# Softmax queries and keys in three bf16 parts instead of two f32r parts, and error attention's loads spread over a batch

## The chip, the cores and the metric

The kernel runs on one core of a Trainium2 chip. The metric is the device time of one execution in microseconds (us); each kernel is timed in several executions and their median is compared. The engines are TensorE (PE), VectorE (DVE), ScalarE (ACT), GpSimd (POOL) and SyncE (SP); SP here issues nearly all transfers, which run on 16 DMA engines.

## The reference, cut to what matters

The input is x of shape (4, 512, 128): four batches (b = 0..3) of 512 tokens. The model adds to x, in this order, half a feed-forward layer with ternary weights, an attention layer, half a feed-forward layer again, half a top-1 mixture of experts, a linear attention, and half the mixture of experts again. The change is in the attention layer, where v is the normalised input itself (16 heads of 8 columns):

```python
scores = jnp.einsum('bhqd,bhkd->bhqk', q, k) * scale          # 16 heads of 8
scores = jnp.where(causal, scores, -jnp.inf)
y_ar = jnp.einsum('bhqk,bhkd->bhqd', jax.nn.softmax(scores, axis=-1), v)
e = v[:, :, 1:, :] - y_ar[:, :, :-1, :]                       # the error of the first attention
...
ma = jnp.einsum('bhqd,bhkd->bhqk', qa, ka)                    # qa from q, ka from other keys, no softmax
ma = jnp.where(jnp.tril(jnp.ones((t - 1, t - 1), dtype=bool)), ma, 0.0)
y_ma = jnp.einsum('bhqk,bhkd->bhqd', ma, e)
out = merge(y_ar) @ w_proj.T + b_proj + (merge(y_ma) @ w_proj.T + b_proj)
```

The softmax is over large scores, so q and k have to enter the products at nearly f32 precision, and the largest score of each query is needed before the exponentials.

## The kernel before, in words

A batch's 512 tokens are NT = 4 tiles of 128. The 16 heads are worked in NS = 4 sets of HL = 4 heads (`hs` = 0..3).

**Split and stack.** PE projects q and k of a batch, ACT copies them to `qf` and `kf` (128 rows, 512 columns). DVE rounds them to f32r (`split`, L1153), POOL subtracts to get the low part (`low`, L590 to L592, called by `low_parts`). SP writes the parts to DRAM with `stack` (L363 to L366), three DMAs of 256 KB for q and three for k, in the orders (high, low, high) and (high, high, low), so that one head has 3 x 8 rows that belong together: high with high, low with high, high with low. A fourth block of 8 rows a head is zero or one, written once at the start (L356 to L361) and used for the row of maxima. The same is done for the features of error attention (`keep_features`). `keep_softmax` and `keep_features` are called batch by batch in SP's program, between the loads of the first sets.

**Sets.** SP loads a set from DRAM, once with queries as weights for the maxima (`load_max_set`, L376 to L382, ring halves 2 and 3) and once with keys as weights for the exponentials (`load_exp_set`, L368 to L374, ring halves 0 and 1): one operand stacked in 128 rows, the other in a block-diagonal ring whose other rows POOL has cleared (`clear_ring`, L573 to L576). A matmul of 128 queries by 4 heads x 128 keys (or the reverse) then gives four heads' scores at once. Maxima: ten such units a set go to PSUM banks, with a causal mask added by a bf16 matmul where the tile is on the diagonal; DVE reduces each (`maxima`, L1164, or two at once, `wide_maxima`, L1173, for the first batch). `max_of_tiles` (L1177 to L1184) joins the tiles, PE turns the result (`max_turn`), ACT copies it (`max_t`), and SP puts the maxima into the ring as the 25th row of a head (`max_row`, L412 to L414; for the very first set ACT does, L941), so that the scores come out with the maximum subtracted.

**Order around the change.** The order of all engines is written out by hand. Ahead of attention: projections and splits of the four batches, the maxima of batch 0, `max_of_tiles(0)`, the first scores. SP's program there is: values and softmax parts of batch 0, the first two maximum sets, features of batch 0, softmax parts and features of batch 1, softmax parts of batch 2, third maximum set, features of batch 2, fourth maximum set, batch 3. In attention, set by set, PE does the scores of a set, the answers of the set before and the maxima of the same set of the next batch; ACT does five exponentials a set (L900), POOL zeroes what is above the diagonals (`clear_late`, L655 to L660), and answers start a set with tile 0's eight matmuls. The last batch has no maxima beside it. At a batch's start SP loads all that error attention needs (`load_state`, L391 to L396: queries 4 x 192 KB, keys 1 MB, the next tokens' values 256 KB) and then the next batch's values (`load_values`, L398 to L402, which waits until the values before have been copied). Error attention of a batch follows its fourth set.

Of the kernel before, what the change touches and what calls it, by code (L numbers as in the profile page):

```python
# [92 lines left out]
SEMS = """held loaded experts_loaded first_loaded xt_low w_abs w_sum w_scale w_half w_low  # L93
w_tern zeroed pad_zero stats moments var_eps rstd normed xt_mm xt_ready x2_mm x2_ready ffn_h ffn_act
ffn_out ffn_base ffn_x x_in0 x_in1 x_in2 x_in3 qkv_mm proj_evac split_hi split_lo q_kept k_kept xset0 xset1 mset0 mset1 v_kept v_in ma_q ma_k
ma_hi ma_lo mq_kept mk_kept state_in ka_t_mm ka_tok v_aug smax_mm smax_red max_t
# [8 lines left out]
MAX_PAIRS = [(qt, kt) for qt in range(NT) for kt in range(qt + 1)]  # L105
EXP_PAIRS = [(kt, qt) for kt in range(NT) for qt in range(kt, NT)]
EXP_UNITS = [((0, 0), (0, 1)), ((0, 2), (0, 3)), ((2, 2), (3, 3)), ((1, 1), (2, 3)), ((1, 2), (1, 3))]
# [9 lines left out]
def build(nc, x_in, bias_cols, w_attn_t, w_k2_t, w_proj_t, b_proj, w1_t, w2_t, b2,  # L117
          l1_w, l1_bv, l1_wp, l1_bp, wr, mw1, mw2, consts, out):
    ctx = ExitStack()
    with ctx:  # L120
# [8 lines left out]
        def unit_slots(i):  # L129
            a, b = (slot_of[pair] for pair in EXP_UNITS[i])  # L130
            return banks[:, a:b + 1:b - a]
# [52 lines left out]
        with nc.sbuf_tensor("sb_xsets", [P, 2, T], F32R) as x_sets:  # L184
            pass
# [10 lines left out]
        yT = w1  # L196
        qs = sb("qs", [P, 2, T], F32R)
        ks = sb("ks", [P, 2, T], F32R)
# [6 lines left out]
        with nc.sbuf_tensor("sb_wide_rows", [P, B, NT, RW], F32) as wide_rows:  # L205
            pass
        ring = sb("ring", [P, NS, HL, T], F32R)
        with nc.sbuf_tensor("sb_v_low", [P, 2, T], F32) as v_low:
            pass
        m_sets = sb("m_sets", [P, 2, T], F32R)  # L210
# [30 lines left out]
        mpart = sb("mpart", [P, NS, NPAIR, HL])  # L241
        mneg = sb("mneg", [P, NT, H])
        mT = qs[0:H, 0]
# [23 lines left out]
        def dram(name, shape):  # L267
            return nc.dram_tensor(name, shape, F32, kind="Internal").ap()

        q_scr = dram("q_scr", [B, H, 4, HD, T])  # L270
        k_scr = dram("k_scr", [B, H, 4, HD, T])
# [14 lines left out]
        def head_rows(scr, b, h, n):  # L286

            return scr[b, h].rearrange("c d t -> (c d) t")[0:n]

        def set_rows(scr, b, hs):  # L290

            return scr[b, HL * hs:HL * hs + HL].rearrange("h c d t -> (h c d) t")
# [43 lines left out]
        def _(sp):  # L336
# [18 lines left out]
            by_set = last_rows(k_scr).rearrange("(s h) d t -> s h d t", h=HL)  # L355
            for dst in (last_rows(q_scr), last_rows(mk_scr), last_rows(k_scr)[:, 1:HD]):  # L356
                n = dst.shape[0] * dst.shape[1] * dst.shape[2] // P
                sp.dma_start(dst, zero[:, 0:n]).then_inc(s["pad_zero"], 16)
            sp.dma_start(by_set[:, 1:HL, 0], zero[0:(HL - 1) * B * NS, 0:T]).then_inc(s["pad_zero"], 16)
            sp.wait_ge(s["zeroed"], 2)  # L360
            sp.dma_start(by_set[:, 0, 0], v_next[0:B * NS].rearrange("p t d -> p (t d)")).then_inc(s["pad_zero"], 16)  # L361
# [5 lines left out]

            def load_exp_set(b, hs):  # L368

                i, done = hs % 2, s[f"xset{hs % 2}"]  # L370
                for hl in range(HL):
                    sp.dma_start(ring[VW * hl:VW * hl + 3 * HD, i, hl].bitcast(F32),
                                 head_rows(q_scr, b, HL * hs + hl, 3 * HD)).then_inc(done, 16)
                sp.dma_start(x_sets[:, i].bitcast(F32), set_rows(k_scr, b, hs)).then_inc(done, 16)  # L374

            def load_max_set(b, hs):  # L376

                i, done = hs % 2, s[f"mset{hs % 2}"]
                for hl in range(HL):
# [4 lines left out]
            def load_features(pad, b, done_q, done_k):  # L384

                for hl in range(HL):
                    dst = pad[VW * hl:VW * hl + 3 * HD, :, hl]
                    sp.dma_start(dst.bitcast(F32), heads(mq_scr[b], hl)).then_inc(done_q, 16)
                sp.dma_start(ka_stk[:].bitcast(F32), sets(mk_scr[b])).then_inc(done_k, 16)

            def load_state(b):  # L391

                hold(sp, s["ym_mm"], NT * b)
                load_features(qa_pad[:].rearrange("p (s h) t -> p s h t", s=NS), b, s["state_in"], s["state_in"])
                sp.dma_start(v_next[:, 0:NT - 1], v_scr[b, 1:T - P + 1].rearrange("(t p) d -> p t d", p=P)).then_inc(s["state_in"], 16)
                sp.dma_start(v_next[0:P - 1, NT - 1], v_scr[b, T - P + 1:T]).then_inc(s["state_in"], 16)  # L396

            def load_values(b):  # L398

                if b:  # L400
                    hold(sp, s["v_aug"], b)
                sp.dma_start(values_of[b % 2][:], v_scr[b].rearrange("(t p) d -> p t d", p=P)).then_inc(s["v_in"], 16)  # L402
# [9 lines left out]
            def max_row(b, hs):  # L412

                sp.dma_start(ring[3 * HD:3 * HD + 1, hs % 2].bitcast(F32),  # L414
                             mT[HL * hs:HL * hs + HL].bitcast(F32)).then_inc(s[f"xset{hs % 2}"], 16)
# [8 lines left out]
            def keep_softmax(b):  # L424

                hold(sp, s["split_lo"], 2 * b + 1)
                stack(qs, q_scr[b], s["q_kept"], (0, 1, 0))
                hold(sp, s["split_lo"], 2 * b + 2)
                stack(ks, k_scr[b], s["k_kept"], (0, 0, 1))
# [8 lines left out]
            sp.wait_ge(s["pad_zero"], 80)  # L438
# [3 lines left out]
            hold(sp, s["q_kept"], 48)  # L442
            hold(sp, s["k_kept"], 48)
# [15 lines left out]
            for kept in ("q_kept", "k_kept"):  # L459
                hold(sp, s[kept], 48 * B)  # L460
            next_max_set(0, 2)
            hold(sp, s["ffn_h"], NF * B)
# [107 lines left out]
        def _(pool):  # L570
            pool.memset(e_pad[:], 0.0).then_inc(s["zeroed"], 1)
            pool.memset(v_next[:], 1.0).then_inc(s["zeroed"], 1)
            pool.memset(carry[:], 0.0).then_inc(s["zeroed"], 1)  # L573
            def clear_ring(first, last):

                pool.memset(ring[:, first:last].bitcast(F32), 0.0).then_inc(s["zeroed"], 1)  # L576
# [17 lines left out]
            def scatter(m, b, first=0, last=NT):  # L594
# [3 lines left out]
                if b == 0 and first == 0:  # L598
                    pool.wait_ge(s["pad_zero"], 80)
# [63 lines left out]
            def errors(b, hs):  # L663

                pool.wait_ge(s["y_norm"], NS * b + hs + 1)
                if hs == 0:
                    pool.wait_ge(s["state_in"], 112 * b + 112)
# [35 lines left out]
            clear_ring(0, 2)  # L703
# [10 lines left out]
            clear_ring(2, 3)  # L714
# [5 lines left out]
            clear_ring(3, 4)  # L720
# [3 lines left out]
            for b in range(1, B):  # L724
                before_attention(b)
            low_parts(B - 1)
# [63 lines left out]
        def _(act):  # L790
# [68 lines left out]
            def max_t(b):  # L859
# [5 lines left out]
                else:  # L865
                    act.wait_ge(s["q_kept"], 48 * B)
# [1244 lines left out]
```

## Time and profile before

| what | value |
|---|---|
| median of 3 executions | 621.57 us (620.26 to 624.51) |
| the profiled execution | 621.04 us |
| its span | 619.2 us |
| mean granted clock of PE | 0.948 |
| PE busy | 505.4 us (82%) |
| DVE busy | 342.3 us (55%) |
| POOL busy | 243.5 us (39%) |
| ACT busy | 214.8 us (35%) |
| DMA | 79.85 MB, mean 129 GB/s |

The span is the time from the first to the last recorded instruction; the rest of the execution's time lies around it. A busy share is an average over stages with different limits, so a stage's limit is read from that stage. The granted clock is PE's, as a share of full speed (2.4 GHz; the lower of its two levels is 1.2 GHz), averaged over a stretch.

### The profile page before, as it was taken

The page shows a single profiled execution, that of the slowest core. Times are in us where ns is not written, and L with a number is a line of the kernel's source. Part 1 is how long each engine was busy: PE and PEld are TensorE (multiplying, and loading weights), DVE is VectorE, ACT ScalarE, POOL GpSimd, SP SyncE. Part 2 cuts the span into 40 slices and gives each one's busy share as a digit, 9 for nine tenths or more (in the row PEclk, how much of TensorE's full clock was granted, in tenths as well). Part 3 has the DMA queues.
Part 4 walks back from the last instruction along what each step waited for, and adds up shares of the span by engine and source line. Part 5 has one row for each costly group of instructions (what it writes and reads, how often), then busy time and mean ns, then how long its engine had stood idle before and what let it go on. Part 6 is the DMA issues. An engine that isn't in the chain of part 4 may idle for free.

```text
span 619.2 us, 10399 instructions
## 1 busy us (share of the span) xinstructions
PE 505.4 (82%) x3827; PEld 322.3 (52%) x3827; DVE 342.3 (55%) x912; ACT 214.8 (35%) x298; POOL 243.5 (39%) x292
## 2 busy tenths in 40 slices
PE   1787787989999999987888878965887788788893
PEld 0664333434644644462467744962456566563692
DVE  5654585648487757751144760323696888842131
ACT  1346331644455455445643701202231311110120
POOL 5667464223342334235332467452220220323153
PEclk9998797989999999998999999997998989977997
DMA  7306999733263263225299523312756273110220
GB/s 261 146 23 198 311 279 298 195 117 95 69 188 96 62 158 118 58 45 155 71 174 217 165 86 111 94 40 72 201 183 187 74 201 111 54 51 35 86 63 10
DMA packets 73666, 79.85 MB, mean 129 GB/s; under 512 B 10946, under 2 KB 50499, under 8 KB 73360
## 3 DMA queue, kind: packets, MB, share of 16 engines
q1 hardware_dynamic: 70760, 73.15, 42.6%
q0 software_dynamic: 2560, 5.58, 2.6%
q8 instruction: 31, 0.51, 0.4%
q10 hardware_dynamic: 296, 0.47, 0.2%
q14 instruction: 19, 0.16, 0.1%
HBM read 44.07 MB, written 35.72 MB: 129 GB/s over the span
## 4 chain that ended last, share of the span: by engine, by line
PE 49%; DVE 17%; SPq 8%; DMA 7%; POOL 7%; issue 6%; ACT 5%; POOLq 0%; DVEq 0%; ACTq 0%
PE ps_accum L1505 15%; PE ps_pair L1505 15%; PE ps_max_pair L1505 13%; SPq L366 3%; POOL sb_rstd L583 2%; DVE sb_stats L1061 2%; DVE sb_work L1400 2%; DMA sb_v_next<-v_scr 2%; DVE sb_mpart L1164 2%; SPq L380 1%; SPq L402 1%; PE ps_turn L1513 1%; POOL xe_scr L603 1%; PE ps_max_pair L1513 1%; DVE sb_mv L1064 1%
## 5 line engine op out<-in xcount | busy, mean ns | idle before, releaser
L1164 DVE TENSOR_REDUCE sb_mpart<-ps_max_pair 128x4 f32<-128x512 f32 x132 | 88.0, 688 | 47.1 <-PE ps_max_pair L1505 46.7
L900 ACT ACTIVATE sb_work<-ps_pair 128x1024 f32<-128x1024 f32 x80 | 80.9, 1024 | 71.3 <-PE ps_pair L1505 70.5
L1505 PE MATMUL ps_max_pair<-sb_ring,sb_m_sets 128*128 128x512 f32 x146 | 64.8, 471 | 7.6 <-DVE sb_mpart L1164 4.6
L660 POOL TENSOR_SCALAR_AFFINE_SELECT sb_work<-sb_work 128x512 f32<-128x512 f32 (+1 forms) x48 | 37.7, 789 | 72.1 <-ACT sb_work L900 72.1
L1505 PE MATMUL ps_pair<-sb_ring,sb_xsets 128*128 128x512 f32 x160 | 58.7, 455 | 8.9 <-DMA sb_ring<-sb_qs 3.7
L1505 PE MATMUL ps_pair<-sb_ident_bf,sb_ones_bf 128*128 128x512 bf16 x185 | 50.6, 431 | 12.3 <-DMA sb_x<-y_scr 8.0
L1505 PE MATMUL ps_accum<-sb_work,sb_v_aug 128*32 128x128 f32 (+3 forms) x768 | 59.3, 408 | 1.1 <-POOL sb_work L660 1.1
L1505 PEld LDWEIGHTS ps_max_pair<-sb_ring,sb_m_sets 128*128 128x128 f32 x146 | 26.9, 191 | 45.1 <-DVE sb_mpart L1164 28.7
L1505 PEld LDWEIGHTS ps_pair<-sb_ring,sb_xsets 128*128 128x128 f32 x160 | 29.0, 200 | 22.6 <-DMA sb_ring<-sb_qs 7.1
L1400 DVE TENSOR_TENSOR sb_work<-ps_pair,sb_cst 128x1024 f32<-128x1024 f32 x32 | 37.5, 1214 | 2.6 <-PE ps_pair L1505 2.6
L1505 PEld LDWEIGHTS ps_pair<-sb_ident_bf,sb_ones_bf 128*128 128x128 bf16 x185 | 19.9, 110 | 36.3 <-issue 11.7
L603 POOL DMA_INDIRECT xe_scr<-sb_exit_rows,sb_slot_all x16 | 15.9, 996 | 54.5 <-DVE sb_slot_all L1145 50.9
L581 POOL TENSOR_SCALAR sb_ve<-sb_mv 128x4 f32<-128x4 f32 x24 | 5.5, 229 | 68.9 <-DVE sb_mv L1064 63.8
L1505 PE MATMUL ps_pair<-sb_y_tmp,sb_mw 128*128 128x256 f32 x128 | 30.7, 383 | 2.0 <-ACT sb_y_tmp L962 2.0
L1505 PEld LDWEIGHTS ps_accum<-sb_work,sb_v_aug 128*32 128x32 f32 x768 | 18.0, 115 | 24.9 <-issue 19.5
L1505 PE MATMUL ps_pair<-sb_xs,sb_w1r 128*128 128x512 f32 x64 | 22.3, 474 | 9.2 <-DVE sb_xs L1080 5.6
L1344 DVE TENSOR_SCALAR sb_work<-ps_pair 128x512 f32<-128x512 f32 x16 | 10.9, 682 | 27.5 <-PE ps_pair L1505 27.5
L1505 PEld LDWEIGHTS ps_pair<-sb_y_tmp,sb_mw 128*128 128x128 f32 x128 | 23.1, 190 | 5.5 <-ACT sb_y_tmp L962 3.0
L583 POOL TENSOR_TENSOR sb_rstd<-sb_ve,sb_cst 128x4 f32<-128x4 f32 x24 | 25.0, 1040 | 2.0
L1505 PE MATMUL ps_pair<-sb_ring,sb_ka_stk 128*128 128x512 f32 x64 | 22.3, 463 | 2.9 <-DVE sb_work L1400 2.8
L679 POOL TENSOR_SCALAR_AFFINE_SELECT sb_work<-sb_work 128x1024 f32<-128x1024 f32 x16 | 17.4, 1091 | 17.5 <-ACT sb_work L891 17.5
L1006 ACT COPY sb_y_tmp<-ps_accum 128x512 f32<-128x512 f32 x16 | 9.4, 586 | 39.8 <-PE ps_accum L1505 39.8
(251 smaller groups left out, 994.6 us busy)
## 6 DMA issues: line engine op xcount, KB each, us to landing
sb_expert_rows<-xe_scr SPq DMA_DIRECT2D x16, 258.0 KB, 2.8
sb_m_sets<-q_scr SPq DMA_DIRECT2D x16, 256.0 KB
sb_ka_stk<-mk_scr SPq DMA_DIRECT2D x4, 1024.0 KB
xe_scr<-sb_cst SPq DMA_DIRECT2D x4, 1024.0 KB, 12.8
sb_mw<-in_mw SPq DMA_DIRECT2D x16, 256.0 KB, 5.9
sb_ka_stk<-mk_scr SPq DMA_DIRECT2D x8, 512.0 KB
sb_xsets<-k_scr SPq DMA_DIRECT2D x15, 256.0 KB
q_scr<-sb_qs SPq DMA_DIRECT2D x12, 256.0 KB, 3.7
```

Of the source, the lines that this page charges most:

```text
L366: sp.dma_start(scr[:, c], hi_lo[:, part, :].bitcast(F32)).then_inc(kept, 16)
L583: pool.tensor_tensor(rstd[i][:], ve[i][:], const("minus_half"), ALU.pow).then_inc(s["rstd"], 1)
L603: pool.indirect_dma_start(xe_scr[m], bass.IndirectOffsetOnAxis(ap=slot_all[:, i:i + 1], axis=0), rows_out[m][b][:, t, :], None).then_inc(s ...
L660: pool.affine_select(weights, weights, [[0, weights.shape[1]], [0, HL], [1, P]], ALU.is_ge, 0.0, base=0, channel_multiplier=-1).then_inc(s ...
L679: pool.affine_select(part, part, [[0, 2 * HL], [1, P]], ALU.is_ge, 0.0, base=-1, channel_multiplier=-1).then_inc(s["ma_zeroed"], 1)
L900: act.activation(unit_slots(i), pair[u % 2][:], ACT.Exp, scale=SCALE).then_inc(s["exp_done"], 1)
L1061: dve.bn_stats(stats[i][:, t, :], src[:, t, :]).then_inc(s["stats"], 1)
L1164: dve.tensor_reduce(mpart[:, m // NPAIR, m % NPAIR, :], max_banks[m % 2][:].rearrange("p (h k) -> p h k", h=HL), AX.X, ALU.max).then_inc(s ...
L1344: dve.tensor_scalar(work[:, n % 2, 1, :], pair[n % 2][:, 1, :], 0.0, None, ALU.max).then_inc(s["h_relu_v"], 1)
L1400: dve.tensor_tensor(work[:, n % 4].rearrange("p a (h q) -> p (a h) q", h=HL), pair[n % 2][:].rearrange("p a (h q) -> p (a h) q", h=HL), bc ...
L1505: return pe.matmul(dst, lhsT, rhs, start=start, stop=stop, skip_group_check=True)
L1513: last = pe.transpose(tile(dst, t), src[:, t, 0:D], ident)
```

## The change

Parts: q and k are split in three bf16 parts each (a, b, c, from high to low). Six products are kept, aa, ab, ac, ba, bb, ca, so a head has 48 rows in place of 24 and two rows of maxima (a bf16 part and the rest) in place of one. Two heads fill 128 rows, at rows 0 and 64, so a set's operands are two head pairs side by side (`x_sets`, `m_sets`, and the rings `x_ring`, `m_ring`, all bf16). PE does as many columns as before, some of them in matmuls of 256.

DVE writes the first part, and POOL's `low_parts` does the rest in six operations, which now wait for DVE's `query_features` as well, since POOL subtracts in place in `qf`. SP writes six DMAs of 128 KB each for q and for k in place of three of 256 KB, loads a set with four DMAs (384 KB in all) in place of five (448 KB), and a row of maxima with two in place of one. Of the zero blocks in DRAM only that of error attention's keys is still written at the start. POOL clears `x_ring` in place of the ring's first half and, behind each of the two other pieces of the ring, half of `m_ring`; it fills `x_sets` with ones before the last batch's split.

Error attention's loads: at a batch's start only the next tokens' values are loaded; the queries come around the maximum set behind set 0, the keys in two halves and the next batch's values behind set 1.

The order of exponentials' units changes in two places: units 2 and 3 are ((2,2),(2,3)) and ((1,1),(3,3)) in place of ((2,2),(3,3)) and ((1,1),(2,3)). `max_of_tiles` gets two more small operations, which split the maxima in two parts.

```diff
+PARTS = 6
+HP = 2
+PR = P // HP
-EXP_UNITS = [((0, 0), (0, 1)), ((0, 2), (0, 3)), ((2, 2), (3, 3)), ((1, 1), (2, 3)), ((1, 2), (1, 3))]
+EXP_UNITS = [((0, 0), (0, 1)), ((0, 2), (0, 3)), ((2, 2), (2, 3)), ((1, 1), (3, 3)), ((1, 2), (1, 3))]
...
+            def stack_queries(b):
+                for c0, c1, part in ((0, 3, 0), (3, 5, 1), (5, 6, 2)):
+                    for c in range(c0, c1):
+                        sp.dma_start(q_scr[b][:, c], q_parts[:, part]).then_inc(s["q_kept"], 16)
+            def stack_keys(b):
+                for c, part in enumerate((0, 1, 2, 0, 1, 0)):
+                    sp.dma_start(k_scr[b][:, c], k_parts[:, part]).then_inc(s["k_kept"], 16)
             def load_max_set(b, hs):
...
-                for hl in range(HL):
-                    sp.dma_start(ring[VW * hl:VW * hl + 3 * HD, 2 + i, hl].bitcast(F32),
-                                 head_rows(k_scr, b, HL * hs + hl, 3 * HD)).then_inc(done, 16)
-                sp.dma_start(m_sets[:, i].bitcast(F32), set_rows(q_scr, b, hs)).then_inc(done, 16)
+                for j in range(HP):
+                    rows_of = slice(PR * j, PR * j + PARTS * HD)
+                    sp.dma_start(m_ring[rows_of, i, :, j], half_rows(k_scr, b, hs, j)).then_inc(done, 16)
+                    sp.dma_start(m_sets[rows_of, i], half_rows(q_scr, b, hs, j)).then_inc(done, 16)
...
             for b in range(B):
-                load_state(b)
-                if b + 1 < B:
-                    load_values(b + 1)
+                load_next_values(b)
                 for hs in range(NS):
...
+                    if hs == 0:
+                        load_queries(b, 0, 2)
                     if b + 1 < B:
                         next_max_set(b + 1, hs)
+                    if hs == 0:
+                        load_queries(b, 2, HL)
+                    elif hs == 1:
+                        load_keys(b, 0, 2)
+                        load_keys(b, 2, NS)
+                        if b + 1 < B:
+                            load_values(b + 1)
...
             def low_parts(b):
-                low(s["split_lo"], qf[:], qs, s["split_hi"], 2 * b + 1)
-                low(s["split_lo"], kf[:], ks, s["split_hi"], 2 * b + 2)
+                operands = ((qf, q_parts), (kf, k_parts))
+                for i, (full, parts) in enumerate(operands):
+                    pool.wait_ge(s["split_hi"], 2 * b + i + 1)
+                    if i == 0:
+                        pool.wait_ge(s["ma_q"], b + 1)
+                    pool.tensor_tensor(full[:], full[:], parts[:, 0], ALU.subtract).then_inc(s["split_part"], 1)
+                for i, (full, parts) in enumerate(operands):
+                    pool.wait_ge(s["split_part"], 4 * b + i + 1)
+                    pool.tensor_copy(parts[:, 1], full[:]).then_inc(s["split_part"], 1)
+                for i, (full, parts) in enumerate(operands):
+                    pool.wait_ge(s["split_part"], 4 * b + i + 3)
+                    pool.tensor_tensor(parts[:, 2], full[:], parts[:, 1], ALU.subtract).then_inc(s["split_lo"], 1)
...
-            clear_ring(2, 3)
+            pool.memset(ring[:, 2].bitcast(F32), 0.0)
+            clear(m_ring[:, 0])
...
-            clear_ring(3, 4)
+            pool.memset(ring[:, 3].bitcast(F32), 0.0)
+            clear(m_ring[:, 1])
...
                 if b:
                     split(b - 1, 0)
+                    query_features(b - 1)
                     split(b - 1, 1)
-                    query_features(b - 1)
...
             def max_of_tiles(b):
...
+                dve.tensor_copy(max_high[:], mneg[:, :, :, 0]).then_inc(s["max_parts"], 1)
+                dve.wait_ge(s["max_parts"], 2 * b + 1)
+                dve.tensor_tensor(mneg[:, :, :, 1], mneg[:, :, :, 0], max_high[:], ALU.subtract).then_inc(s["max_parts"], 1)
...
             def scores(b, u):
...
                 for a in range(2):
-                    kt, qt = EXP_UNITS[i][a]
-                    last = mm(pair[u % 2][:, a, :], tile(x_sets[:, hs % 2], kt), ring[:, hs % 2, :, qt * P:(qt + 1) * P])
+                    if one_key_tile(i):
+                        kt, qt = EXP_UNITS[i][0]
+                        last = mm(pair[u % 2][:, a, :], tile(k_of[:, a], kt), q_of[:, a, :, qt * P:(qt + 2) * P])
+                    else:
+                        kt, qt = EXP_UNITS[i][a]
+                        for p in range(HP):
+                            last = mm(pair[u % 2][:, a, p * 2 * P:(p + 1) * 2 * P], tile(k_of[:, p], kt),
+                                      q_of[:, p, :, qt * P:(qt + 1) * P], start=p == 0)
```

## Rows read from the trace of the kernel before

**Rows 1.** Busy time by stretch: us, busy (count) by engine, PE clock, DMA share, GB/s.

```profile
60.00:78.00 18.00, 13.71 (x53) 7.73 (x52) 10.76 (x26) 5.21 (x9) 8.76 (x9) 0.81 0.98 311
78.00:106.00 28.00, 21.65 (x72) 9.21 (x71) 20.70 (x24) 7.40 (x12) 16.26 (x9) 0.90 0.92 296
...
168.00:222.60 54.60, 52.09 (x414) 28.24 (x412) 38.31 (x73) 27.92 (x31) 20.18 (x28) 1.00 0.42 115
```

**Rows 2.** Chain of waits within one set of attention: start us, us, what.

```profile
192.66 0.67 PE ps_pair L1505 x2
...
194.80 0.46 PE ps_pair L1505 x2
```

**Rows 3.** Chain of waits, whole run, three of its long pieces.

```profile
112.81 7.87 SPq L402
...
276.61 11.31 DMA sb_v_next<-v_scr
...
554.31 5.83 PE ps_pair L1505 x27
```

**Rows 4.** Timeline of PE: first answers of successive sets, and one waiting pair of scores.

```profile
119.86 1.06 PE L1505 MATMUL ps_accum<-sb_work,sb_v_aug 128*32 128x512 f32 x8
...
134.52 1.07 PE L1505 MATMUL ps_accum<-sb_work,sb_v_aug 128*32 128x512 f32 x8
...
189.16 1.06 PE L1505 MATMUL ps_accum<-sb_work,sb_v_aug 128*32 128x512 f32 x8
...
198.89 1.06 PE L1505 MATMUL ps_accum<-sb_work,sb_v_aug 128*32 128x512 f32 x8
...
283.92 1.06 PE L1505 MATMUL ps_accum<-sb_work,sb_v_aug 128*32 128x512 f32 x8
...
289.54 1.22 PE L1505 MATMUL ps_pair<-sb_ring,sb_xsets 128*128 128x512 f32 x2 [3.14 <-POOL sb_work L660]
...
295.74 1.07 PE L1505 MATMUL ps_accum<-sb_work,sb_v_aug 128*32 128x512 f32 x8
...
301.95 1.06 PE L1505 MATMUL ps_accum<-sb_work,sb_v_aug 128*32 128x512 f32 x8
```

**Rows 5.** Timeline of SP's queue: start us, us to issue, line, transfer, count.

```profile
49.61 1.93 SPq L366 DMA_DIRECT2D k_scr<-sb_ks  x3
...
58.99 1.81 SPq L366 DMA_DIRECT2D mq_scr<-sb_feat  x3
...
82.75 0.35 SPq L382 DMA_DIRECT2D sb_m_sets<-q_scr  x1
...
279.95 5.70 SPq L372 DMA_DIRECT2D sb_ring<-q_scr  x4
```

**Rows 6.** Groups by line and form: weight loads in f32 and bf16.

```profile
L1505 PEld LDWEIGHTS ps_max_pair<-sb_ring,sb_m_sets 128*128 128x128 f32 x146 | 26.9, 191 | 45.1 <-DVE sb_mpart L1164 28.7 <-issue 9.1 <-DVE sb_mpart L1173 3.1
...
L1505 PEld LDWEIGHTS ps_max_pair<-sb_add_q_bf,sb_ident_bf 128*128 128x128 bf16 x59 | 5.7, 96 | 12.2 <-issue 10.9
```

**Rows 7.** Timeline of POOL: a clearing, batch 0's split, a copy.

```profile
38.90 1.81 POOL L576 MEMSET sb_ring<- 128x2048 f32 x1
...
45.57 1.99 POOL L592 TENSOR_TENSOR sb_qs<-sb_qf,sb_qs 128x512 fp32r<-128x512 f32 x1 [1.56 <-DVE sb_qs L1153]
47.52 1.27 POOL L592 TENSOR_TENSOR sb_ks<-sb_kf,sb_ks 128x512 fp32r<-128x512 f32 x1
...
99.55 0.61 POOL L652 COPY sb_v_aug<-sb_values 128x512 f32<-128x512 f32 x1
```

**Rows 8.** Timeline of PE: the first matmul of the maxima and the first scores.

```profile
59.46 0.50 PE L1505 MATMUL ps_max_pair<-sb_ring,sb_m_sets 128*128 128x512 f32 x1 [0.78 <-DMA sb_m_sets<-q_scr]
...
106.05 1.19 PE L1505 MATMUL ps_pair<-sb_ring,sb_xsets 128*128 128x512 f32 x2 [0.29 <-DMA sb_ring<-sb_qs]
```

**Rows 9.** Timeline of DVE: the last double reduction and the four that join tiles.

```profile
99.47 1.22 DVE L1173 TENSOR_REDUCE sb_mpart<-ps_max_pair 128x8 f32<-128x1024 f32 x1
100.72 0.55 DVE L1182 TENSOR_REDUCE sb_mneg<-sb_mpart 128x16 f32<-128x16 f32 x4
```

More of the change, by code:

```diff
@@ L130, in unit_slots, with one_key_tile, unit_scores @@
             a, b = (slot_of[pair] for pair in EXP_UNITS[i])
-            return banks[:, a:b + 1:b - a]
+            slots = banks[:, a:b + 1:b - a]
+            return slots.rearrange("p n (h q) -> p h n q", h=HL) if one_key_tile(i) else slots
+        def one_key_tile(i):
+            a, b = EXP_UNITS[i]
+            return a[0] == b[0]
+        def unit_scores(u):
+            if one_key_tile(u % NG_X):
+                return pair[u % 2][:].rearrange("p a (j n q) -> p (a j) n q", j=HP, n=2)
+            return pair[u % 2][:]
         def diagonal_slots(i):
@@ L196, in build @@
         yT = w1
+        with nc.sbuf_tensor("sb_q_parts", [P, 3, T], BF16) as q_parts:
+            pass
+        with nc.sbuf_tensor("sb_max_rows", [P, T], BF16) as max_rows:
+            pass
         qs = sb("qs", [P, 2, T], F32R)
+        with nc.sbuf_tensor("sb_k_parts", [P, 3, T], BF16) as k_parts:
+            pass
         ks = sb("ks", [P, 2, T], F32R)
@@ L354, in _ @@
             zero = e_pad[:].rearrange("p t h v -> p (t h v)")
[L355 to L361, printed above, removed]
+            n = B * H * HD * T // P
+            sp.dma_start(last_rows(mk_scr), zero[:, 0:n]).then_inc(s["pad_zero"], 16)
             def stack(hi_lo, scr, kept, order):
@@ L391, in load_state, with load_queries @@
-            def load_state(b):
+                for j in range(HP):
+                    rows_of = slice(PR * j, PR * j + PARTS * HD)
+                    sp.dma_start(m_ring[rows_of, i, :, j], half_rows(k_scr, b, hs, j)).then_inc(done, 16)
+                    sp.dma_start(m_sets[rows_of, i], half_rows(q_scr, b, hs, j)).then_inc(done, 16)
+            def load_queries(b, first, last):
+                for hl in range(first, last):
+                    dst = qa_pad[VW * hl:VW * hl + 3 * HD].rearrange("p (s h) t -> p s h t", s=NS)[:, :, hl]
+                    sp.dma_start(dst.bitcast(F32), heads(mq_scr[b], hl)).then_inc(s["state_in"], 16)
@@ L393, in load_state, with load_keys, load_next_values @@
+            def load_keys(b, first, last):
+                sp.dma_start(ka_stk[:, first:last].bitcast(F32), sets(mk_scr[b])[:, first:last]).then_inc(s["state_in"], 16)
+            def load_next_values(b):
                 hold(sp, s["ym_mm"], NT * b)
-                load_features(qa_pad[:].rearrange("p (s h) t -> p s h t", s=NS), b, s["state_in"], s["state_in"])
-                sp.dma_start(v_next[:, 0:NT - 1], v_scr[b, 1:T - P + 1].rearrange("(t p) d -> p t d", p=P)).then_inc(s["state_in"], 16)
@@ L412, in max_row @@
             def max_row(b, hs):
-                sp.dma_start(ring[3 * HD:3 * HD + 1, hs % 2].bitcast(F32),
-                             mT[HL * hs:HL * hs + HL].bitcast(F32)).then_inc(s[f"xset{hs % 2}"], 16)
+                for j in range(HP):
+                    r = PR * j + PARTS * HD
+                    sp.dma_start(x_ring[r:r + 2, hs % 2, :, j], max_of_heads(hs, j)).then_inc(s[f"xset{hs % 2}"], 16)
             def keep_values(b):
@@ L899, in attention @@
                         act.wait_ge(s["pv_mm"], STEPS * b + NT * (hs - 1) + LAST_OF_UNIT[i] + 1)
-                    act.activation(unit_slots(i), pair[u % 2][:], ACT.Exp, scale=SCALE).then_inc(s["exp_done"], 1)
+                    act.activation(unit_slots(i), unit_scores(u), ACT.Exp, scale=SCALE).then_inc(s["exp_done"], 1)
                     if hs and i == 1:
@@ L940, in _ @@
             act.wait_ge(s["max_t_evac"], 1)
-            act.dma_start(ring[3 * HD:3 * HD + 1, 0].bitcast(F32), mT[0:HL].bitcast(F32)).then_inc(s["xset0"], 16)
+            for j in range(HP):
+                r = PR * j + PARTS * HD
+                act.dma_start(x_ring[r:r + 2, 0, :, j], max_of_heads(0, j)).then_inc(s["xset0"], 16)
             act.wait_ge(s["mq_kept"], 48 * B)
```

190 lines of the change are left out of this document (105 added, 85 removed).

## The prediction

> **What bounds the kernel now.** The profiled execution took 621.0 us, of which the span is 619.2 and 1.8 lie around it; it stands 0.5 below the median of 621.57, so a difference found on it is carried to the median as it is. I read first the busy time by stage [rows 1]: in 168.0 to 222.6, attention in full flow, PE is busy 52.1 of 54.6 us, DVE 38.3, the DMA engines 0.42. So a set of four heads costs what PE costs there. From 60 to 106, ahead of attention, PE isn't the bound: the DMA share is 0.98 and then 0.92, the granted clock 0.81 and 0.90. Then the chain of waits inside one set: all PE. A pair of score matmuls there costs 0.46 us [rows 2], but 0.67 where it follows the answers' matmuls, whose weights had to be in the array until then.
>
> The same chain over the whole run has a few long pieces in the attention [rows 3]: 7.87 us in which SP can't hand over its load of the next values, and 11.31 us in which the load of the next tokens' values lands. The starts of successive sets' first answers [rows 4] show what these cost. Undisturbed, a set takes 198.89 - 189.16 = 9.73. The disturbed set of the first batch takes 134.52 - 119.86 = 14.66: a loss of 4.9. In the last batch, which computes no maxima beside its scores, the sets take 301.95 - 295.74 = 6.21, the disturbed one 295.74 - 283.92 = 11.82: a loss of 5.6. There SP's four loads for a set took 5.70 us to issue [rows 5] behind the load of queries, keys and next values, and the scores of that set waited 3.14 us, to 289.54.
>
> **The stalls.** The change leaves only the 256 KB of next values at a batch's start; queries follow set 0, keys and values set 1, so the sets' loads are issued ahead of the big ones. In the last batch the set that was late would be issued at 280 and land by about 285, before the 286.4 (289.54 - 3.14) at which its scores are due; the 1 MB of keys then has two sets of time. I take both losses off: **-10.5** (bounds -10.5 and 0, if the sets still queue behind something).
>
> **The sets.** Scores and maxima read bf16 operands of the same 128 partitions. PE streams bf16 columns in 5.83 / 27 = 0.216 us for 512 (the third row of [rows 3], matmuls of a bf16 identity), against 0.46 / 2 = 0.23 [rows 2]. Loading weights takes 96 ns in bf16 and 191 in f32 [rows 6]; of that some 5 loads a set stand open. 20 matmuls x 0.013 + 5 x 0.095 = 0.74; the cut of some matmuls into two of 256 columns (4 + 2 more a set, each with a weight load that may open) gives 0.2 back: 0.5 a set. 12 sets beside maxima: 6.0. The last batch's four have a pitch of 6.21 with the five exponentials of a set close behind on ACT: half of it, 0.25 each, 1.0. **-7.0**, bounds -3 (the streaming alone) and -9 (nothing given back); DVE's reductions read the same columns as before.
>
> POOL's zeroing of unit 3 now covers two diagonals and unit 2's one; the answers that need them come last in their set, two exponentials later, which covers it; without that cover it would be under half a microsecond a set.
>
> **Ahead of attention.** Here the change adds, and nothing runs beside it that could hide it.
> (1) POOL's clearing: behind the f32 piece of 1.81 us [rows 7] comes a second, bf16, of equally many elements, twice on the way to batch 0's split. At half the time or the full time each: 1.8 to 3.6, less some 0.5 idle: taken 2.1, bounds 1.3 and 3.0.
> (2) The split: POOL's start waits for one more DVE operation (+0.6, an estimate from the copy of the same 128x512 on POOL, 0.61), and q's last part is the fifth of six operations: 1.99 + 1.27 + 0.61 + 0.61 + 1.27 = 5.75 by the subtractions and the nearest copy [rows 7], instead of 1.99. +3.8. The writes start at 47.6 + 2.1 + 0.6 + 3.8 = 54.1.
> (3) The writes to DRAM: q and k take six each in place of three; each carries half the bytes. SP spent 1.93 on k's three and 1.81 on the features' three [rows 5], 0.60 to 0.64 each; the first three met an idle queue and the others a filling one, and they differ by little, so I take it as the price of issuing and not of bytes: 12 x 0.60 = 7.2, to 61.3 instead of 51.5 (49.61 + 1.93). k's earlier readiness doesn't help: it stands behind q's writes on SP's queue.
> (4) Loads of the first maxima's set: four instead of five (-0.35), 64 KB less, and the last write lands with half the bytes: the first maxima's matmul, at 59.46 before [rows 8], 7.9 after the last write's issue, comes 6.2 after it, at about 67.5, **+8.0**.
> PE has little else ready and waits some 6 us; after such waits the granted clock was 0.81 [rows 1], worth up to 2 more until the projection of the second batch.
> (5) The same chain holds for batch 2, whose split and writes stand ahead of the loads of the third set of maxima on SP's queue: +4 on POOL, +3.2 on SP (six writes more, less a half of one that waited anyway). That set's last load was handed over at 83.1 [rows 5] and landed at about 86 (7.9 us are two landings and 1.9 of issue, so 3.0 each); now at 86 + 8 + 4 + 3.2 = 101, or 99 to 103 by the clock. From it the last ten double reductions run at 1.22 [rows 9]: 12.2, to 113. From the last reduction's end, 100.7, to the first scores, 106.05, it was 5.35; two more small operations (+0.45, from four in 0.55 [rows 9]) and a second issue for the rows of maxima (+0.65, near a write's) make 6.45: 113 + 6.45 is 119.5; first scores at about 119, **+13**. Bounds: +7 (issue in proportion to bytes, short memsets, clock held) and +18 (0.75 a write under load, long memsets, a cold clock twice).
> The zero writes of about 2 MB at the start that go end long before anything waits for them: 0, and so do DVE's merged waits for the weights' scale.
>
> **Between batches.** Three more times the two small operations stand ahead of the next batch's maxima rows: 3 x 0.45 = **+1.4** (bounds 0 and +2). The doubled issue there is covered by a set's pitch.
>
> **The sum:** 621.0 - 10.5 - 7.0 + 13 + 1.4 = 617.9; predicted 618, in effect the same time. Less than 1% either way (615.4 to 627.8 about the median) is what a measurement of this kernel can't tell from no change.
>
> **Rivals.**
> (a) *Writes cost by bytes.* If the 0.60 us is DMA time and not SP's, twelve half-sized writes cost what six did: steps 3 and 5 lose 3.6 + 3.2, the start of attention comes at +6, and the time is 611. For it: the DMA share of 0.98 [rows 1] in the stretch where most writes lie. Against it: the rows of 0.60 to 0.64, of which the first met an idle queue. Chance 0.30.
> The Trainium skill (DMA: Bandwidth & Descriptors, "Issuing engines are not separate DMA queues") says that the sequencer's time to start a DMA is "usually small relative to the DMA itself"; by that rule this rival holds; the rows of 0.60 us agree only if those 0.60 are the DMA's own.
> (b) *The split becomes the bound of the whole approach.* Each of batches 0 to 2 needs its own chain of split and writes before the next may overwrite q and k: 4.4 + 3.6 = 8 a batch, three in a row, first scores at +24. Nothing in attention changes: 621.0 + 24 - 16.1 = 629. It decides from first scores later than 129 (then -16.1 is outweighed by more than 22.9). For it: the DMA share of 0.98 and 0.92 up to 106 [rows 1], so that no batch's writes find an idle queue. Against: batch 1's split has slack, since PE has the first two sets of maxima to do meanwhile. Chance 0.14.
> (c) *The stalls stay*, since the split loads of queries and keys meet the sets' loads later: 617.9 + 10.5 = 628. Chance 0.06.
> (d) *bf16 gives nothing in a set*, because each PSUM bank's reduction on DVE (38.3 of 54.6 us) sets the pace, or the loads of weights were hidden: 617.9 + 7.0 = 625. For it: DVE's share; against: the chain of a set holds no DVE piece [rows 2]. Chance 0.06.
> The Trainium skill (TensorE: Matmul & The Clock Gate, "Step-by-step: what each phase is for") has the next weights load while the current matmul runs; by that rule the shorter load would give nothing, as in (d). The pair of 0.67 against 0.46 disagrees for the matmuls behind the answers.
>
> **How the numbers follow.** The forecast has 0.44 by itself, 610 (+7, -9) to 627 (+18, -3) in its own range. Faster by over 1%: rival (a) and 0.04 of the forecast, 0.34. Slower by over 1%: (b) and half of (c), 0.17. Within: 0.49. The range 608 to 629 reaches from just below (a) to (b).
>
> **What would show it.** Issue of a 128 KB write: 0.60 (right) or 0.3 (rival a). First maxima at about 67, first scores at 119: later than 129 is rival (b). Sets at 9.2 in batches 0 to 2, 9.7 is rival (d). No pieces of SP's hand-over and of next values in the chain, pitches of the first and last batch even; otherwise (c). The forecast is wrong in its centre if the bf16 clearing or the six POOL operations run at other speeds than their f32 neighbours, most simply if a bf16 copy or subtraction is half as long.

## The result and the profile after

The changed kernel takes 628.37 us in the median (625.84 to 631.82, 7 runs), the kernel before 621.57 (617.18 to 624.51, 7 runs): a ratio of 1.0119, 95% interval 1.0078 to 1.016. It is slower by 1.2%. The time lies inside the range that was forecast, but the side was missed: 618, no difference, was forecast. The profiled execution took 627.64 us, 6.6 more than that of before; its span is 625.9.

```profile
span 625.9 us, 10628 instructions
...
PE 490.5 (78%) x3923; PEld 304.1 (49%) x3923; DVE 341.8 (55%) x920; ACT 213.2 (34%) x298; POOL 260.5 (42%) x311
```

PE has 15 us less to do and POOL 17 more. Where the time went is read from two stretches: up to the first scores, and from there on.

**Up to the first scores.** Timelines of POOL (batch 0's clearing and split), of SP's queue (the writes) and of PE (maxima and first scores); they answer to [rows 7], [rows 5] and [rows 8].

```profile
41.55 1.80 POOL L618 MEMSET sb_m_ring<- 128x2048 bf16 x1
...
48.88 1.21 POOL L678 TENSOR_TENSOR sb_qf<-sb_qf,sb_q_parts 128x512 f32<-128x512 f32 x1 [2.23 <-DVE sb_qaf L1215]
...
52.30 1.15 POOL L684 TENSOR_TENSOR sb_q_parts<-sb_qf,sb_q_parts 128x512 bf16<-128x512 f32 x1
```

```profile
53.54 3.78 SPq L393 DMA_DIRECT2D q_scr<-sb_q_parts  x6
57.43 3.77 SPq L398 DMA_DIRECT2D k_scr<-sb_k_parts  x6
```

```profile
67.27 0.39 PE L1577 MATMUL ps_max_pair<-sb_m_ring,sb_m_sets 128*128 128x512 bf16 x1 [4.42 <-DMA sb_m_sets<-q_scr]
...
101.36 1.04 PE L1577 MATMUL ps_pair<-sb_m_ring,sb_m_sets 128*128 128x512 bf16 x2 [5.18 <-DMA sb_m_sets<-q_scr]
...
109.07 0.61 PE L1577 MATMUL ps_max_pair<-sb_m_ring,sb_m_sets 128*128 128x512 bf16 x2 [1.39 <-DMA sb_m_sets<-q_scr]
...
123.11 1.87 PE L1577 MATMUL ps_pair<-sb_x_ring,sb_xsets 128*128 128x512 bf16 x4 [3.75 <-DMA sb_x_ring<-sb_max_rows]
```

The bf16 clearing costs as much as the f32 one. The split begins at 48.88 in place of 45.57, its fifth operation at 52.30, the queries' six writes at 53.54, and six writes take 3.78 us, 0.63 each. The first maxima come at 67.3, the third set lands at 101.4 and the first scores stand at 123.11 in place of 106.05: 17.1 us later.

**From the first scores on**, the kernel is faster: 513.2 us of span remained before (619.2 - 106.05), 502.8 remain now. The starts of first answers, in answer to [rows 4]:

```profile
137.32 1.06 PE L1577 MATMUL ps_accum<-sb_work,sb_v_aug 128*32 128x512 f32 x8
...
146.85 1.06 PE L1577 MATMUL ps_accum<-sb_work,sb_v_aug 128*32 128x512 f32 x8
...
201.28 1.07 PE L1577 MATMUL ps_accum<-sb_work,sb_v_aug 128*32 128x512 f32 x8
...
210.81 1.06 PE L1577 MATMUL ps_accum<-sb_work,sb_v_aug 128*32 128x512 f32 x8
...
295.60 1.06 PE L1577 MATMUL ps_accum<-sb_work,sb_v_aug 128*32 128x512 f32 x8
302.68 1.07 PE L1577 MATMUL ps_accum<-sb_work,sb_v_aug 128*32 128x512 f32 x8
...
309.82 1.06 PE L1577 MATMUL ps_accum<-sb_work,sb_v_aug 128*32 128x512 f32 x8
```

The first batch's disturbed set fell from 14.66 to 9.53, the last batch's from 11.82 to 7.08: the stalls are gone. But a set that wasn't disturbed fell only from 9.73 to 9.53, and in the last batch it rose from 6.21 to 7.14 (a set's pitch: from its first answers to those of the next). The chain of waits inside a set, in answer to [rows 2], shows why: it is no longer all PE.

```profile
203.40 0.17 DVE sb_rcp L1288
...
203.59 0.30 DVE sb_y_ar L1290
...
203.97 0.46 POOL sb_e_pad L724
204.43 0.41 POOL sb_v_next L725
204.84 1.06 POOL sb_work L712
...
206.03 0.42 PE ps_accum L1577 x8
```

DVE divides the answers of the set before, POOL subtracts them twice for the error, then zeroes unit 3 (now two diagonals, 1.06), and the answers of tile 3, third of four, wait for it. Before the change it was tile 1's answers, the last, that needed unit 3 zeroed.

### The profile page after: what moved, and what is told of

It reads as the page before. It is cut to its first block, busy times and chain, and to the rows that moved or that the text cites. A ratio compares the mean times of both kernels' runs of the same rounds, so it can differ in the third digit from the quotient of the medians.

```text
span 625.9 us, 10628 instructions
## 1 busy us (share of the span) xinstructions
PE 490.5 (78%) x3923; PEld 304.1 (49%) x3923; DVE 341.8 (55%) x920; ACT 213.2 (34%) x298; POOL 260.5 (42%) x311
## 4 chain that ended last, share of the span: by engine, by line
PE 44%; DVE 18%; POOL 12%; issue 8%; DMA 7%; ACT 6%; SPq 5%; POOLq 0%; ACTq 0%; DVEq 0%
PE ps_accum L1577 14%; PE ps_pair L1577 14%; PE ps_max_pair L1577 11%; POOL sb_work L712 2%; DVE sb_work L1472 2%; DVE sb_stats L1119 2%; POOL sb_rstd L625 2%; ACT sb_work L956 1%; DVE sb_mpart L1229 1%; SPq L393 1%; PE ps_turn L1585 1%; POOL xe_scr L645 1%; DVE sb_mpart L1226 1%; SPq L398 1%; DMA sb_m_sets<-q_scr 1%
## 5 line engine op out<-in xcount | busy, mean ns | idle before, releaser
L1229 DVE TENSOR_REDUCE sb_mpart<-ps_max_pair 128x2 f32<-128x512 f32 x106 | 71.0, 688 | 40.0 <-PE ps_max_pair L1577 38.5
L1577 PE MATMUL ps_max_pair<-sb_m_ring,sb_m_sets 128*128 128x512 bf16 (+1 forms) x176 | 55.4, 353 | 13.3 <-DMA sb_m_sets<-q_scr 5.8
L1577 PE MATMUL ps_accum<-sb_work,sb_v_aug 128*32 128x128 f32 (+3 forms) x768 | 57.7, 398 | 9.7 <-POOL sb_work L712 8.5
L1577 PE MATMUL ps_pair<-sb_ident_bf,sb_ones_bf 128*128 128x512 bf16 x185 | 47.9, 413 | 12.3 <-DMA sb_x<-y_scr 8.0
L1577 PE MATMUL ps_pair<-sb_x_ring,sb_xsets 128*128 128x512 bf16 (+1 forms) x192 | 48.9, 355 | 6.2 <-DMA sb_x_ring<-sb_max_rows 4.1
L1577 PEld LDWEIGHTS ps_max_pair<-sb_m_ring,sb_m_sets 128*128 128x128 bf16 x176 | 15.5, 99 | 53.4 <-DVE sb_mpart L1229 23.0
L1577 PEld LDWEIGHTS ps_pair<-sb_x_ring,sb_xsets 128*128 128x128 bf16 x192 | 16.5, 99 | 26.6 <-issue 11.8
L1577 PE MATMUL ps_max_pair<-sb_add_q_bf,sb_ident_bf 128*128 128x256 bf16 (+1 forms) x88 | 27.6, 314 | 0.0
```

Source lines behind the costliest of these rows:

```text
L1229: dve.tensor_reduce(mpart[:, slot, h:h + HP, p], bank.rearrange("p (j k) -> p j k", j=HP), AX.X, ALU.max).then_inc(s["smax_red"], 1)
L1577: return pe.matmul(dst, lhsT, rhs, start=start, stop=stop, skip_group_check=True)
```

## The experiments

Two theories stand against each other for the sets: A, POOL's zeroing of unit 3 behind its subtractions sets the pace; B, DVE's reductions or the short matmuls do. For the start, the question is how much of the 17 us the writes, the clearing and the late fourth set each take.

**The old units (e1).**

```diff
-EXP_UNITS = [((0, 0), (0, 1)), ((0, 2), (0, 3)), ((2, 2), (2, 3)), ((1, 1), (3, 3)), ((1, 2), (1, 3))]
+EXP_UNITS = [((0, 0), (0, 1)), ((0, 2), (0, 3)), ((2, 2), (3, 3)), ((1, 1), (2, 3)), ((1, 2), (1, 3))]
```

> The changed kernel with the exponentials' units 2 and 3 as before, ((2,2),(3,3)) and ((1,1),(2,3)); one diagonal is zeroed behind the error subtractions instead of two. Theory A (POOL's zeroing of unit 3 sets the pace of a set): batch 1's pitch falls from 9.53 to 9.2-9.3 us, the last batch's from 7.14 to 6.0-6.2, the time from 628.4 to about 622 (ratio to the kernel before 1.001). Rival B (reductions on DVE or the short matmuls set the pace): pitches stay at 9.5-9.7 and 7.1, time 628 or more, since two more matmuls a set are cut in two.

621.40 us, ratio to the kernel before 1.0009 (0.9981 to 1.0037): 7 us back. PE's first answers, two sets of batch 1 and three of the last batch:

```profile
198.47 1.06 PE L1577 MATMUL ps_accum<-sb_work,sb_v_aug 128*32 128x512 f32 x8
...
207.40 1.07 PE L1577 MATMUL ps_accum<-sb_work,sb_v_aug 128*32 128x512 f32 x8
...
289.73 1.07 PE L1577 MATMUL ps_accum<-sb_work,sb_v_aug 128*32 128x512 f32 x8
...
295.62 1.06 PE L1577 MATMUL ps_accum<-sb_work,sb_v_aug 128*32 128x512 f32 x8
...
303.24 1.06 PE L1577 MATMUL ps_accum<-sb_work,sb_v_aug 128*32 128x512 f32 x8
```

A set of batch 1 takes 8.93, 0.80 less than before the change, although two more matmuls a set are cut in two. The last batch's next to last pitch is 5.89. The last is 7.62, which theory A didn't foresee: in the chain of waits the maxima rows of set 3, issued behind the queries' load, took 5.42 us to land. Theory A holds; the pitch fell further than it forecast.

**Zeroing ahead of the subtractions (e2)**, the same cause taken away in another place:

```diff
                     clear_late(b, hs, 1)
-                    errors(b, hs - 1)
                     clear_late(b, hs, 2)
+                    errors(b, hs - 1)
```

> The changed kernel with POOL's zeroing of unit 3 put ahead of its two error subtractions, nothing else. Theory A: the 0.87 us of subtractions and the wait for DVE's division leave the chain; batch 1's pitch 9.53 to 9.0-9.3, the last batch's 7.14 to 6.0-6.3, time 621-623. Rival B: pitches unchanged, 628.

623.33 us, ratio 1.0022 (0.9982 to 1.0062). Batch 1's pitch, between these two rows, is again 8.93, with the changed units kept:

```profile
201.18 1.06 PE L1577 MATMUL ps_accum<-sb_work,sb_v_aug 128*32 128x512 f32 x8
...
210.11 1.06 PE L1577 MATMUL ps_accum<-sb_work,sb_v_aug 128*32 128x512 f32 x8
```

So it is the order on POOL, and not the units' shapes for PE, that had kept the sets at 9.53. From its first scores (125.49) to its end this run takes 496.1 us, and the old units take 496.2 (618.8 - 122.56). What it is slower by lies ahead of attention, where its execution's granted clock was lower (0.69 from 60 to 78, against 0.88).

**Spread loads alone (e3)**, on the kernel before:

```diff
-                load_state(b)
-                if b + 1 < B:
-                    load_values(b + 1)
+                load_next_values(b)
...
+                    if hs == 0:
+                        load_queries(b, 0, 2)
                     if b + 1 < B:
                         next_max_set(b + 1, hs)
+                    if hs == 0:
+                        load_queries(b, 2, HL)
+                    elif hs == 1:
+                        load_keys(b, 0, 2)
+                        load_keys(b, 2, NS)
+                        if b + 1 < B:
+                            load_values(b + 1)
...
```

> The kernel before with the loads of error attention spread as in the change, and nothing else of it (f32r in two parts stays). Theory A (the stalls came from the order of loads alone): both disturbed sets fall to 9.7 and 6.2, time 621.6 - 10.5 = 611 (ratio 0.983). Rival B (the f32r sets of 448 KB still queue behind queries and keys, the stall goes only with the smaller bf16 sets): 617 or more.

611.20 us, ratio 0.9817 (0.9784 to 0.985). The first scores, and the disturbed sets of the first and of the last batch:

```profile
107.23 0.93 PE L1514 MATMUL ps_pair<-sb_ring,sb_xsets 128*128 128x512 f32 x3
...
120.55 1.07 PE L1514 MATMUL ps_accum<-sb_work,sb_v_aug 128*32 128x512 f32 x8
...
130.28 1.06 PE L1514 MATMUL ps_accum<-sb_work,sb_v_aug 128*32 128x512 f32 x8
...
279.63 1.07 PE L1514 MATMUL ps_accum<-sb_work,sb_v_aug 128*32 128x512 f32 x8
...
285.83 1.07 PE L1514 MATMUL ps_accum<-sb_work,sb_v_aug 128*32 128x512 f32 x8
```

9.73 and 6.20, the undisturbed pitches. From the first scores to the end 502.7 us remain (609.9 - 107.23), 10.5 less than before. Half of the change alone beats both kernels, and the other half costs 17 us on top of it.

**The loads put back (e4)**, on the changed kernel (the same edit the other way round, with the stricter wait for the values' copy):

> The changed kernel with error attention's loads and the next values back at a batch's start, all parts in bf16 as changed. Theory A: the stalls return, one disturbed set in the first batch (14 us instead of 9.5) and one in the last (11-12 instead of 7.1): 628.4 + 9 = 637 (ratio 1.025). Rival B (bf16 sets of 384 KB escape the stall): 628.

646.23 us, ratio 1.0379 (1.0328 to 1.0429). Its chain of waits has the pieces of [rows 3] again:

```profile
132.51 7.22 SPq L436
142.65 4.83 DMA sb_x_ring<-sb_max_rows
...
300.29 5.18 SPq L405
307.61 5.06 DMA sb_x_ring<-sb_max_rows
```

The stalls return, and larger than expected (15.8 and 14.6 us for the two sets). Behind the blocked queue, too, the maxima rows land late (4.83 and 5.06 us). Smaller bf16 sets don't escape the stalls. The two sets make 13.7 of the 19.0 us by which the span grew; of the rest, 1.8 lie ahead of the first scores and 2.9 behind the last set, and their cause wasn't looked for.

**The clearing moved (e5, e10)** (on the changed kernel with the old units, 621.4, as all that follow):

```diff
...
-            pool.memset(ring[:, 2].bitcast(F32), 0.0)
...
-            pool.memset(ring[:, 3].bitcast(F32), 0.0)
...
             values(0)
+            pool.memset(ring[:, 2:4].bitcast(F32), 0.0)
```

> As the changed kernel with the old units (621.4 us), and the two f32 clearings of the ring (1.80 us each) that stand ahead of batch 0's split moved behind it, to just before attention. Theory A (the doubled clearing is on the path to the first scores): the split starts 2.6 us earlier (46.2), the first maxima at 64.6, the first scores at 119-120 instead of 122.6; 618 (ratio 0.995). Rival B (something else holds the split by then): 621.

621.55 us, ratio 1.0009 (0.9976 to 1.0043): nothing gained. The first maxima came 3.1 us earlier, at 64.2, and yet the first scores at 122.61, where the old units alone had 122.56. DVE's timeline and POOL's have the loss:

```profile
113.42 2.99 DVE L1254 CAST sb_max_high<-sb_mneg 128x64 bf16<-128x64 f32 x1
```

```profile
112.84 3.52 POOL L785 MEMSET sb_ring<- 128x4096 f32 x1
```

DVE's cast of 64 columns took 2.99 us and ended at 116.41, as POOL's moved clearing ended at 116.36. A rival explanation is that PE ran at a lower clock. So the same clearing was put elsewhere, into the first mixture of experts:

> As e5_clears_moved (the changed kernel with the old units and the ring's two f32 clearings taken off the path of batch 0's split), but these clearings stand in the first mixture of experts and not just ahead of attention. Theory A (e5 lost its gain because DVE's cast waited for the moved clearing): the cast of the maxima takes 0.2 instead of 2.99, first scores at 119.5 instead of 122.6, 618.5 (ratio 0.995). Rival B (the earlier start is lost to PE's lower clock): 621.5.

618.85 us, ratio 0.9959 (0.9933 to 0.9985).

```profile
114.05 0.19 DVE L1253 CAST sb_max_high<-sb_mneg 128x64 bf16<-128x64 f32 x1
```

The cast is back at 0.19, the first scores are 2.0 earlier, at 120.61, and the median is 2.6 lower than with the old units. So the doubled clearing costs 2 to 2.6 us. The intervals of e5 and e10 just overlap; what tells the two apart is the trace. From the end of the last reduction to the issue of the maxima rows on ACT's queue it is 2.27 us with the old units (115.74 to 118.01), 2.68 in e10 (113.55 to 116.23) and 5.48 in e5 (112.91 to 118.39). Of e5's 3.2 more, 2.8 are the cast; the other 0.4 is PE's turn of the maxima, 1.03 in place of 0.61 at a lower granted clock (0.81 from 106 to 120, against 1.00), and e10 has that too.

**Three writes in place of six (e6).** The rows of a head in another order, so that parts that lie side by side go in one transfer (keys alike, with their parts in reverse):

```diff
...
-                for c0, c1, part in ((0, 3, 0), (3, 5, 1), (5, 6, 2)):
-                    for c in range(c0, c1):
-                        sp.dma_start(q_scr[b][:, c], q_parts[:, part]).then_inc(s["q_kept"], 16)
+                for c0, c1 in ((0, 3), (3, 5), (5, 6)):
+                    sp.dma_start(q_scr[b][:, :, c0:c1].rearrange("h d c t -> (h d) c t"), q_parts[:, 0:c1 - c0]).then_inc(s["q_kept"], 16)
...
```

> As the changed kernel with the old units (621.4 us), and the six 128 KB writes of q and of k each joined to three (384, 256 and 128 KB, the rows of a head in another order, the same bytes). Theory A (a write costs SP 0.63 us to issue whatever it carries): three take 1.9 instead of 3.78, the first maxima come at 63.5 instead of 67.3, the first scores at 115-116 instead of 122.6; 614.5 (ratio 0.989). Rival B (issue goes with bytes): a three takes 3.6 and nothing moves, 621.

613.58 us, ratio 0.9862 (0.9817 to 0.9907): 7.8 us less than with the old units alone (6.3 between the profiled executions). SP's queue, and PE's first scores:

```profile
53.89 1.33 SPq L392 DMA_DIRECT2D q_scr<-sb_q_parts  x3
55.33 1.94 SPq L397 DMA_DIRECT2D k_scr<-sb_k_parts  x3
```

```profile
115.57 1.87 PE L1576 MATMUL ps_pair<-sb_x_ring,sb_xsets 128*128 128x512 bf16 x4 [1.78 <-DMA sb_x_ring<-sb_max_rows]
```

Batch 0's same 768 KB are issued in 1.33 or 1.94 us in place of 3.78, and the first scores stand 7.0 earlier than with the old units alone (122.56). The joined writes also move longer pieces (78,532 DMA packets in the whole run in place of 81,988), and no run halves the number of writes without that; SP's rows show the time of issue itself. An unasked cost: in the last batch set 3 now comes at 296.71 - 287.09 = 9.62, its maxima rows later still behind the queries.

**The fourth set's loads ahead of the features' writes (e7):**

```diff
             next_max_set(0, 0)
-            keep_features(2)
             next_max_set(0, 1)
+            keep_features(2)
```

> As the changed kernel with the old units (621.4 us), and the loads of the fourth set of maxima put ahead of the third batch's feature writes on SP's queue. Theory A (the last reductions ahead of attention also wait for that set, 1.4 us): first scores 1.5 earlier, 620 (ratio 0.998). Rival B (the writes come back later as a wait of the features): 621.4.

622.80 us, ratio 1.0017 (0.9987 to 1.0047), no gain, the first scores at 124.37. The wait of 1.39 for the set is gone, but here too DVE's cast ran into a clearing, the 6.92 us that stood there already:

```profile
115.84 1.44 DVE L1255 CAST sb_max_high<-sb_mneg 128x64 bf16<-128x64 f32 x1
```

```profile
110.31 6.92 POOL L784 MEMSET sb_qa_pad<- 128x8192 f32 x1
```

It ended at 117.28, the clearing at 117.23. Step by step, from the third set's first matmul to the last reduction's end it is 13.67 us (101.67 to 115.34), 0.8 less than with the old units (101.30 to 115.74): that is what the earlier set gives. From there to the issue of the maxima rows it is 4.26 (to 119.60) in place of 2.27: 1.25 more for the cast, 0.32 for the subtraction behind it (0.55 beside POOL's copy, in place of 0.23), and 0.43 for PE's turn (1.04 in place of 0.61; the granted clock from 106 to 120 was 0.85, with the old units 1.00).

**All of it together (e8, e9)**, with the bf16 clearings in POOL's idle time at the start and the keys of the last batch a set later:

> Old units, f32 clearings moved, the two bf16 clearings moved to POOL's idle time at the start, three writes for q and for k, fourth set ahead of the features' writes, and in the last batch the keys of error attention loaded a set later. If the parts add: 621.4 - 3 - 1.8 - 7 - 1.5 - 1.5 = 606.6 (ratio 0.976), below the spread loads alone (611.2). If they overlap on SP's queue: 611 or more.

609.25 us, ratio 0.982 (0.9778 to 0.9863). Not the full sum: the cast took 2.27 us, up to 106.22, beside the pad's clearing (99.25 + 6.92 = 106.17), and the last batch's maxima rows landed late again, as its chain of waits has them:

```profile
103.95 2.27 DVE L1254 CAST sb_max_high<-sb_mneg 128x64 bf16<-128x64 f32 x1
```

```profile
99.25 6.92 POOL L782 MEMSET sb_qa_pad<- 128x8192 f32 x1
```

```profile
283.43 4.97 DMA sb_x_ring<-sb_max_rows
```

So both were taken away: the pad's clearing waits for DVE's split of the maxima, the ring's goes to the mixture of experts, and the last batch's queries load behind set 3's rows.

```diff
...
-            pool.memset(qa_pad[:].bitcast(F32), 0.0).then_inc(s["zeroed"], 1)
             pool.wait_ge(s["zeroed"], 8)
             values(0)
+            pool.wait_ge(s["max_parts"], 2)
+            pool.memset(qa_pad[:].bitcast(F32), 0.0).then_inc(s["zeroed"], 1)
...
```

> As e8_all (609.25 us), with three moves. The f32 clearing of the ring's halves 2 and 3 goes to the first mixture of experts, and the 6.93 us clearing of the error attention's query pad behind DVE's split of batch 0's maxima. In the last batch the queries load after set 1, behind set 3's maxima rows. Theory A (DVE's cast to bf16 ends only when POOL's clearing ends; the maxima rows of the last set queue behind the queries): the cast takes 0.2 instead of 2.27 us, first scores at 110.5 instead of 112.7, the last batch's last pitch 5.9 instead of 7.15; 606 (ratio 0.976). Rival B (the cast was slow for another reason, the rows are late anyway): 609.

605.86 us, ratio 0.975 (0.9719 to 0.9781): faster than both kernels, and below the spread loads alone. The first scores and the last batch's last pitch:

```profile
108.53 1.02 PE L1578 MATMUL ps_pair<-sb_x_ring,sb_xsets 128*128 128x512 bf16 x4 [2.00 <-DMA sb_x_ring<-sb_max_rows]
```

```profile
280.76 1.06 PE L1578 MATMUL ps_accum<-sb_work,sb_v_aug 128*32 128x512 f32 x8
...
286.61 1.06 PE L1578 MATMUL ps_accum<-sb_work,sb_v_aug 128*32 128x512 f32 x8
```

## Why the prediction was wrong

**The stalls (-10.5): right.** 4.9 came back in the first batch. The last batch's 5.6 came back as well, but a new wait took 0.9 from each of two sets there. The spread loads alone gave 10.5 from the first scores on (e3), and rival (c) is out. The reason was right too: the order on SP's queue, and not the sets' size (e4).

**The sets (-7.0): the step that failed.** From the first scores to the end the span shrank by 10.4; with 10.5 for the stalls and 1.4 for the operations between batches (a batch's last first answers to the next batch's: 24.92 to 25.39 twice, 24.64 to 25.06), 1.3 is what remains for the sets. The failing sentence is that POOL's zeroing of unit 3 lies "two exponentials later, which covers it". With the changed units, tile 3's answers, third and not last, need unit 3. And the zeroing isn't behind the exponential alone: on POOL's queue it stands behind two subtractions that wait for DVE's division, and it became late with them. "Under half a microsecond a set" was 0.6 in batches 0 to 2 (9.53 to 8.93) and about 1.2 in the last (7.08 to 5.89). With that wait gone (e1), the rest of the span from the first scores is 496.2, 16.9 less than before, where -16.1 had been forecast. The gain of bf16 was put at 0.5 a set and is 0.8. The weights' part is seen in e1's chain:

```profile
201.27 0.35 PE ps_accum L1577 x8
201.62 0.54 PE ps_pair L1577 x2
...
203.38 0.43 PE ps_pair L1577 x2
```

Behind the answers a pair of scores now costs 0.54, elsewhere 0.43: the open load fell from 0.21 [rows 2] to 0.11. The Trainium skill's rule of weights that load during the matmul before (TensorE: Matmul & The Clock Gate, "Step-by-step: what each phase is for") doesn't hold in full for these pairs. Rival (d) had nearly the right pace (9.7) for the wrong reason: its bf16 gain is there, POOL's order hid it.

**Ahead of attention (+13): mis-sized, it was +17.1.** Step by step: clearing 2.65 (POOL's next operation from 42.65 to 45.30; taken 2.1, bf16 at the f32's time, the upper half of the bounds); the writes 5.9 later (6.5), the POOL operations up to the fifth taking 4.57 (48.88 to 53.45) and not 5.75; the issue of a write 0.63 (taken 0.60), so that rival (a) is out; the first maxima at 67.3 (67.5); the third set at 101.4 (101). That these last two fit so well is in part luck: the clearing and the writes were taken too short, the POOL operations too long. Nearly all of the miss comes behind that. The ten reductions took 14.65 from that set's first matmul to the last one's end (101.36 to 116.01), not 12.2. Ten times 1.22 leaves out the start: before the change the last ten took 13.2 by the same count (87.50 to 100.69). The fourth set landed late (1.39 us of wait), since the features' writes stood ahead of it on SP's queue; loaded earlier, it gave back 0.8 (e7). And the first pair of maxima took 1.04 in place of 0.61, PE having idled 5.18 us (below: from 78 to 106 the granted clock was 0.76, a mean of the levels of 1.2 and 2.4 GHz, against 0.90 in [rows 1]). The way from there to the scores took 7.1 and not 6.45, as two issues of maxima rows on ACT's queue take 1.89. Rounding 119.5 down to 119 was another half. Busy time by stretch, in answer to the second of [rows 1]:

```profile
78.00:106.00 28.00, 19.62 (x64) 8.23 (x64) 16.13 (x22) 8.00 (x13) 18.02 (x17) 0.76 0.76 222
```

The Trainium skill has the start of a DMA as "usually small relative to the DMA itself" (DMA: Bandwidth & Descriptors, "Issuing engines are not separate DMA queues"). For one write the trace bears this out, 0.63 us of SP for 128 KB that land 2.4 us after their issue (median); for six in a row it doesn't, as they hold SP for 3.78 us, longer than one takes to land, and with half as many the kernel took 7.8 us less.

**Rival (b)** is out by its own point: the first scores came at 123, not later than 129. The side was lost by two terms that missed the same way: 5.7 us in the sets and 4.1 ahead of them. Together they use up the 9.8 between the forecast of 618 and the upper 1%.

**What stays open:** how much of e6's gain is the number of writes and how much the longer pieces that they move; and what made the rest of e4's loss beside its two stalled sets.

## What to carry to other kernels

Cost a moved or grown operation by all that stands ahead of it on its own queue, and by the first reader of what it writes: here one mask, put behind two subtractions, ate five sixths of what faster matmuls had earned. Count transfers as well as bytes: here, where a queue hands them over one by one ahead of a critical stage, joining them gave 7.8 us, as much as bf16 gave all the sets once nothing stood in its way (e1). Where a change has two halves that touch different stages, time each alone.

## What was not expected of the hardware

A DVE cast from f32 to bf16 that began while POOL cleared memory did not end before the clearing. The cast of 128x64 took 0.19 us beside an idle POOL, and 1.44, 2.27 and 2.99 when a clearing ran, ending each time within 0.06 us of its end; the reductions beside the same clearings kept their 1.22. The larger cast of the split shows the same in the changed kernel, 1.10 in place of 0.43, and ends 0.27 behind the clearing (DVE's timeline, then POOL's):

```profile
94.95 1.10 DVE L1211 CAST sb_q_parts<-sb_qf 128x512 bf16<-128x512 f32 x1 [2.21 <-DMA q_scr<-sb_q_parts]
```

```profile
93.97 1.81 POOL L781 MEMSET sb_xsets<- 128x2048 bf16 x1
```

It isn't the clearing alone: beside one of POOL's subtractions (84.31 to 85.46) that cast took 0.99, to 85.75. A clearing of 2048 elements a partition took 1.80 us in bf16 and in f32: half the bytes, the same time.
